# Two PSUM buffers in turn for the query, gate and attention products of a fused attention and feed-forward block

## What is computed

```python
x = x + _layernorm(attn(_layernorm(x)))
x = x + _layernorm(ffn(_layernorm(x)))

def attn(x):                        # 16 heads of 64
    q = elu(x @ Wq + bq) + 1;  k = elu(x @ Wk + bk) + 1;  v = x @ Wv + bv
    kv = einsum('bhsd,bhse->bhde', k, v)     # 64 x 64 for each head
    a = einsum('bhsd,bhde->bhse', q, kv)
    return (sigmoid(x @ Wg + bg) * a) @ Wo + bo
```

## Time and profile before

| | us |
|---|---|
| median of the 2 runs | 8979.28 |
| the two runs | 8975.19, 8983.37 |
| the profiled execution | 8972.89 |
| its span on the slowest core (core 4) | 8971.4 |
| its spans on the 8 cores | 8903.2 to 8971.4 |

### The profile page before, as it was taken

The page is one execution under the profiler, slowest core; times in us unless marked ns, Lnnn a source line. Parts: engine busy times, 40 slices in busy tenths (PEclk is TensorE's granted clock), DMA queues, the critical chain, the costliest instruction groups (busy, mean ns, idle before and its releaser), DMA issues.

```text
span 8971.4 us, 65942 instructions; the slowest of 8 cores (8903.2 to 8971.4 us)
## 1 busy us (share of the span) xinstructions
PE 3763.7 (42%) x20044; PEld 2064.9 (23%) x20044; DVE 2859.9 (32%) x5319; ACT 1023.5 (11%) x1615; POOL 386.6 (4%) x214
## 2 busy tenths in 40 slices
PE   0246566563767667765232213222332132213221
PEld 0122222222444444443111111111111111111110
DVE  4521211213222222222433343234323432343333
ACT  0211111110111111111001010101010101010101
POOL 0200000000000000000000000000000000000000
PEclk9987777776888888887666667665756676667676
DMA  6610000002000000001232223222322232223221
GB/s 187 198 51 19 19 24 19 21 22 75 19 24 29 29 29 27 17 29 38 63 85 62 57 51 85 63 57 49 85 59 59 52 85 61 59 50 85 61 61 45
DMA packets 679993, 495.11 MB, mean 55 GB/s; under 512 B 561891, under 2 KB 561891, under 8 KB 677606
## 3 DMA queue, kind: packets, MB, share of 16 engines
q1 hardware_dynamic: 660198, 423.78, 17.9%
q0 software_dynamic: 19456, 67.12, 2.1%
HBM read 423.71 MB, written 67.11 MB: 55 GB/s over the span
## 4 chain that ended last, share of the span: by engine, by line
PE 35%; DVE 26%; DMA 17%; issue 9%; ACT 8%; POOL 3%; DVEq 2%; SPq 0%; ACTq 0%; POOLq 0%
DMA w2qs<-w2q 7%; DMA w1qs<-w1q 6%; PE pq L724 5%; PE pk L520 5%; PE po L822 4%; PE pg L759 4%; PE ph L1244 4%; PE pv L520 4%; POOL H L1131 3%; DVE H L1051 3%; DVE H L1048 3%; ACT H L1057 2%; PE po2a L1165 2%; DVE H L1043 2%; PE po2b L1165 2%
## 5 line engine op out<-in xcount | busy, mean ns | idle before, releaser
L1244 PE MATMUL ph<-xqT,w1qs 128*128 128x256 bf16 x4096 | 571.4, 303 | 351.0 <-DMA w1qs<-w1q 317.9
L1165 PE MATMUL po2a<-w2qs,hqb 128*128 128x512 bf16 x1024 | 374.3, 453 | 791.1 <-DMA w2qs<-w2q 400.0
L1090 PE MATMUL pbcst<-identf,cmaxb 128*128 128x128 f32 x64 | 28.6, 447 | 1483.9 <-DVE cmaxb L1084 1454.5
L1244 PEld LDWEIGHTS ph<-xqT,w1qs 128*128 128x128 bf16 x4096 | 428.1, 108 | 494.1 <-issue 406.8
L1253 DVE TENSOR_TENSOR H<-ph,invB 128x256 f32<-128x256 f32 x512 | 217.6, 425 | 701.6 <-PE ph L1244 701.2
L1131 POOL TENSOR_TENSOR H<-H,sc2B 128x8192 f32<-128x8192 f32 x16 | 257.2, 16076 | 3032.8 <-DVEq L109 3032.8
L1165 PE MATMUL po2b<-w2qs,hqb 128*128 128x512 bf16 x1024 | 384.3, 464 | 0.0
L1185 DVE TENSOR_SCALAR ffnb<-po2a,fac2c 128x1024 f32<-128x1024 f32 x16 | 20.5, 1284 | 1071.2 <-PE po2b L1165 1071.2
L1090 PEld LDWEIGHTS pbcst<-identf,cmaxb 128*128 128x128 f32 x64 | 11.7, 182 | 1500.8 <-issue 1500.8
L724 PE MATMUL pq<-xh_b,wq_h 128*128 128x256 f16 x1024 | 169.8, 321 | 408.5 <-DVE qf L737 328.2
L1014 PE MATMUL pbcst<-diagb,onesf 128*128 128x128 f32 x64 | 24.5, 487 | 712.1 <-DVE diagb L1010 712.1
(11 more groups left out here) (206 smaller groups left out, 6969.1 us busy)
## 6 DMA issues: line engine op xcount, KB each, us to landing
w1qs<-w1q SPq DMA_DIRECT2D x256, 512.0 KB, 4.4
w2qs<-w2q SPq DMA_DIRECT2D x512, 256.0 KB, 2.6
qstage<-w SPq DMA_DIRECT2D x64, 512.0 KB, 4.4
qstage<-w SPq DMA_DIRECT2D x16, 2048.0 KB, 9.9
xin<-x SPq DMA_DIRECT2D x32, 512.0 KB, 3.6
xr_b<-x SPq DMA_DIRECT2D x32, 512.0 KB, 4.3
x<-x_b POOLq DMA_DIRECT2D x32, 512.0 KB, 5.9
x2in<-x SPq DMA_DIRECT2D x16, 1024.0 KB, 5.3
```

What stands on the lines that cost most here:

```text
L1165: last = t.matmul(out=PO2[tl][:, half * 512:(half + 1) * 512], lhsT=hqb[:, s, tl * 128:(tl + 1) * 128], rhs=w2qs[:, wb, half * 512:(half + ...
L1244: last = t.matmul(out=pb[:, :], lhsT=w1qs[:, (s // 2) % 2, s % 2, c, :], rhs=xqT[:, buf, c, :], start=(c == 0), stop=(c == 7))
```

## The change

Each of the three tiles `pq`, `pg` and `pa` becomes two tiles, and the chunks take them in turn (`fo % 2`, `pr % 2`). The free event is kept for each tile, so a chunk waits for the readers of the chunk two before it and no longer of the one before it. Nothing else is changed: the same instructions stand in the same order in all five lists. PSUM tiles are placed by whole banks of 2 KB; phase 2 had 3 tiles in one bank each and `po` in two, and has 6 and two after.

```diff
-        pq = ps2("pq", [128, 256])
-        pg = ps2("pg", [128, 256])
-        pa = ps2("pa", [128, 256])
+        pq2 = [ps2("pq0", [128, 256]), ps2("pq1", [128, 256])]
+        pg2 = [ps2("pg0", [128, 256]), ps2("pg1", [128, 256])]
+        pa2 = [ps2("pa0", [128, 256]), ps2("pa1", [128, 256])]
...
-        pq_free = Res()
-        pg_free = Res()
-        pa_free = Res()
+        pq_free = [Res(), Res()]
+        pg_free = [Res(), Res()]
+        pa_free = [Res(), Res()]
...
+                pq = pq2[fo % 2]
...
-                p.op("tensor", q_mm, wait=[t_xT, t_wqgo] + pq_free.wait(), inc=[s_qmm2.inc()])
+                p.op("tensor", q_mm, wait=[t_xT, t_wqgo] + pq_free[fo % 2].wait(), inc=[s_qmm2.inc()])
...
-                pq_free.freed_by((s_qch, s_qch.v))
+                pq_free[fo % 2].freed_by((s_qch, s_qch.v))
...
+                pg = pg2[fo % 2]
...
-                p.op("tensor", g_mm, wait=[t_xT, t_wqgo] + pg_free.wait(), inc=[s_gmm.inc()])
+                p.op("tensor", g_mm, wait=[t_xT, t_wqgo] + pg_free[fo % 2].wait(), inc=[s_gmm.inc()])
...
-                pg_free.freed_by((s_gch, s_gch.v))
+                pg_free[fo % 2].freed_by((s_gch, s_gch.v))
...
+                pa = pa2[pr % 2]
...
-                p.op("tensor", a_mm, wait=[t_q, t_kv] + pa_free.wait(), inc=[s_amm.inc()])
+                p.op("tensor", a_mm, wait=[t_q, t_kv] + pa_free[pr % 2].wait(), inc=[s_amm.inc()])
...
-                pa_free.freed_by((s_gav, s_gav.v))
+                pa_free[pr % 2].freed_by((s_gav, s_gav.v))
```

More of the change, by code:

```diff
@@ L718, in build_nc, with q_mm @@
             for fo in range(8):
-                def q_mm(t, fo=fo, buf=buf):
+                pq = pq2[fo % 2]
+                def q_mm(t, fo=fo, buf=buf, pq=pq):
                     last = None
@@ L728, in q_mm @@
                     return last
-                p.op("tensor", q_mm, wait=[t_xT, t_wqgo] + pq_free.wait(), inc=[s_qmm2.inc()])
+                p.op("tensor", q_mm, wait=[t_xT, t_wqgo] + pq_free[fo % 2].wait(), inc=[s_qmm2.inc()])
                 t_qmm = (s_qmm2, s_qmm2.v)
-                p.op("vector", lambda v, fo=fo: v.tensor_scalar(
+                p.op("vector", lambda v, fo=fo, pq=pq: v.tensor_scalar(
                     out=qtmp[:, :], in0=pq[:, :], scalar1=bqcol[:, fo:fo + 1], scalar2=0.0,
@@ L753, in build_nc, with g_mm @@
             for fo in range(8 if KP2SUB >= 2 else 0):
-                def g_mm(t, fo=fo, buf=buf):
+                pg = pg2[fo % 2]
+                def g_mm(t, fo=fo, buf=buf, pg=pg):
                     last = None
@@ L763, in g_mm @@
                     return last
-                p.op("tensor", g_mm, wait=[t_xT, t_wqgo] + pg_free.wait(), inc=[s_gmm.inc()])
+                p.op("tensor", g_mm, wait=[t_xT, t_wqgo] + pg_free[fo % 2].wait(), inc=[s_gmm.inc()])
                 t_gmm = (s_gmm, s_gmm.v)
-                p.op("scalar", lambda sE, fo=fo: sE.activation(
+                p.op("scalar", lambda sE, fo=fo, pg=pg: sE.activation(
                     out=gT[:, fo, :], in_=pg[:, :], func=AF.Sigmoid, bias=bgcol[:, fo:fo + 1],
@@ L769, in build_nc, with a_mm @@
                     wait=[t_gmm] + gT_free[fo].wait(), inc=[s_gch.inc()])
-                pg_free.freed_by((s_gch, s_gch.v))
+                pg_free[fo % 2].freed_by((s_gch, s_gch.v))
             xTb_free[buf].freed_by((s_qmm2, s_qmm2.v), (s_gmm, s_gmm.v))
             for pr in range(8 if KP2SUB >= 3 else 0):
-                def a_mm(t, pr=pr):
+                pa = pa2[pr % 2]
+                def a_mm(t, pr=pr, pa=pa):
                     c0 = pr * 128
@@ L789, in a_mm @@
                                     tile_position=(64, 64))
-                p.op("tensor", a_mm, wait=[t_q, t_kv] + pa_free.wait(), inc=[s_amm.inc()])
+                p.op("tensor", a_mm, wait=[t_q, t_kv] + pa_free[pr % 2].wait(), inc=[s_amm.inc()])
                 t_amm = (s_amm, s_amm.v)
-                p.op("vector", lambda v, pr=pr: v.scalar_tensor_tensor(
+                p.op("vector", lambda v, pr=pr, pa=pa: v.scalar_tensor_tensor(
                     out=qf32[:, pr, :], in0=pa[:, :], scalar=1.0, in1=gT[:, pr, :],
```

## The result

| | before | after |
|---|---|---|
| median of the runs, us | 8979.19 (10 runs) | 8484.37 (11 runs) |
| ratio after / before | | 0.944, 95% interval 0.941 to 0.947 |
| the profiled execution's span, us | 8971.4 | 8475.9 |
| mean of its spans on the 8 cores, us | 8949.4 | 8449.2 |

The change makes the kernel 5.6% faster. This and every later ratio leaves out executions in which the cores of one die ran at a lower clock than the others and took longer (2 of the 11 of the changed kernel, 8605 and 8743 us).

What follows compares the result with a forecast made beforehand. Waits bound the kernel, no engine being busy for half the span. Gains of 15 x 32.2 + 30.5 = 513 us, taken from 8972.9, give 8459.9; the runs' median lies 6.4 higher: 8466 us, range 8425 to 8570.

Steps and rivals of the forecast that it cites:

- Chunk 2 starts where chunk 1 did, slowly: Q stage: chunk 2 still waits for the LN in VectorE's queue, starting at 3090.53; TensorE idles 5.6 us instead of 8.11.
- VectorE is the bound from there at 3.28 us: Q stage from chunk 2's data on: VectorE's chain takes 3.28 us a chunk, of which TensorE works 2.62.
- Full clock from chunk 3: Q stage: TensorE runs at 2.4 GHz from chunk 3 on, 2.62 us a chunk.
- Bound (a): Q stage, clock of chunk 3: at 1.2 GHz VectorE starts it 2.1 us later, +34 us; chunk 2 already fast, -5 us.
- bound (b): Q stage: one more slow chunk in the steady part costs 1.8 us, +29 us in all.
- The a stage keeps VectorE's pace: A stage: 8 x 1.45 us and about 0.2 us, 11.8 us against 13.1 or 13.4; gain 1.4 us an iteration.
- The o stage stays as it is: O stage: unchanged, since its own wait concerns po, which is not doubled; no gain or loss.
- Bound (c): O stage start: if a shorter a stage kept the clock up, about 2.2 us would be won, -35 us in all.
- A (q stays slow): Rival, q stage: stays at 1.2 GHz, 5.1 us a chunk; 8645 us; chance 0.10 including cases between it and the forecast.
- B (no gain): Rival, q and g stages: denser work is granted 1.2 GHz throughout; 8960 us, or 8979 us; chance 0.05.
- C (slower): Rival: q, g and o stages all at 1.2 GHz, 18 us more an iteration in o; about 9250 us; chance 0.03.
- D (the clock sags in part): Rival: a quarter of g and o matmuls at 1.2 GHz, 9.5 us an iteration, 152 us; 8618 us; chance 0.03.

Runs made afterwards that it cites:

- two casts: The changed kernel with VectorE's cast into q_hb done three times instead of once in each q chunk: ratio 0.948 to the kernel before.
- filled gaps: The kernel before, single tiles, with extra matmuls into an unread PSUM tile behind q chunks 0 to 6: 8888 us against 9014, ratio 0.983.
- later profile: The changed kernel run again unaltered, as base for other runs: 8521 us against 9041 for the kernel before, ratio 0.944.
- `pq` alone: The changed kernel with only pq doubled, pg and pa single again: 8687 us against 9014 for the kernel before, ratio 0.962.
- mixed a stage: The changed kernel with its six tiles as one pool and attention products placed between g chunks: 8339 us against 9041 before, ratio 0.917.
- `pa` alone: The changed kernel with only pa doubled, pq and pg single again: 8989 us against 9014 for the kernel before, ratio 0.996.
- `pg` alone: The changed kernel with only pg doubled, pq and pa single again: 8877 us against 9014 for the kernel before, ratio 0.984.

## Why the prediction was right, step by step

All times here are put on the iteration of the timeline of after: its first q matmul at 2947.05 stands for 3079.64 in the prediction, 132.59 us earlier.

- *Chunk 2 starts where chunk 1 did, slowly.* Forecast 2957.94, measured 2957.95; idle 5.6 us forecast, 5.49 measured; its end forecast 2962.8, measured 2963.01.
- *VectorE is the bound from there at 3.28 us.* It starts at 2963.26 where 2963.0 was forecast, then at 2966.54 and 2969.82: 3.28 us. The two casts show that it is the bound and not only a match.
- *Full clock from chunk 3.* 1.00 in the window; the slow rows are of chunk 2 alone. Bound (a) and bound (b) did not occur here. (Bound (a) was summed a little high: 3095.4 + 5.1 + 0.24 is 1.8 us behind 3098.9, not 2.1.) The sign "granted clock of the q stage above 0.9" was just missed: 0.89 for the stage as a whole, because of chunk 2 and the idle time ahead of it. That the clock follows the gaps, which the prediction took from the comparison of q and g, is shown by the filled gaps.
- *The g stage has no wait.* Forecast 2977.3 to 2998.5, measured 2977.60 to 2998.73.
- *The a stage keeps VectorE's pace.* The first L795 forecast at 2999.36, measured at 2999.59; the pace is 1.45 us. The o stage starts at 3011.83 and not at 3011.16: 0.2 us are inherited, and in this iteration VectorE loses 0.46 us before its last operation.
- *Reading one tile while the other is written costs nothing.* The first read of `pq` takes 0.48 us before and after. The term put at nothing was nothing.
- *The o stage stays as it is.* Not quite, and this is the largest miss in the sum. Bound (c), a faster start, did not come true; the start is slower. The first eight matmuls take 3.57 us as in the earlier trace rows, but the second eight of the iteration read take longer, before (core 4) and after (core 6):

```profile
3056.17 2.44 PE L822 MATMUL po<-wo_l,gav_h 128*128 128x512 f16 x8
```

```profile
3015.20 2.91 PE L825 MATMUL po<-wo_l,gav_h 128*128 128x512 f16 x8
```

The forecast was built on one iteration of each stage. The means of 14 iterations (the second to the fifteenth, same cores; us, rounded) show what that cost:

| from first start to first start | before, the iteration used | before, mean | after, forecast | after, mean |
|---|---|---|---|---|
| q stage | 53.2 | 53.2 | 30.3 | 30.7 |
| g chunks 0 to 6 | 26.1 | 26.6 | 18.3 | 18.4 |
| g chunk 7 and a stage | 17.0 | 16.9 | 15.5 | 15.6 |
| o stage | 26.8 | 26.9 | 26.8 | 27.4 |
| iteration | 123.2 | 123.6 | 91.0 | 92.1 |

The iteration after is 1.1 us longer than forecast: 0.4 us in the q stage, 0.5 in the o stage, where the trace has 5.6 us at 1.2 GHz against 4.6 before, and 0.1 in the a stage. But the mean iteration before is 0.5 us longer than the one used, mostly because 4 of 16 g stages restart slowly. The two misses partly cancel, and that is luck: the gain is 31.5 us and not 32.2. The first iteration, put at 30.5 us with half of the late start as a guess, gave 30.0 (mean start of its o stage over the cores, 2308.2 us before and 2278.2 after). Together that is 10 us less than the forecast of 513. The other 8 us between 8466 and 8484 are no step of the sum; they are less than what phase 3 differs by between cores and runs.

*The rivals.* A (q stays slow) is refuted by `pq` alone and the window. B (no gain) and C (slower) by the result. D (the clock sags in part) was set aside too firmly. In the profiled execution of after it is not there, but in the same kernel's later profile six cores had it in this stretch, two of them for a quarter of the time, see the last section. The figure that the Trainium skill (TensorE: Matmul & The Clock Gate, Part 1) gives for it, 13/16, is the level that the later profiles show, and the row of phase 1 that I held against it, 216 ns a matmul, shows only that it does not always come: the profiled executions of before and after have no time at 0.81 on any core.

## What to carry to other kernels

A single PSUM tile between TensorE and a slow chain costs twice: the waits themselves, and the clock that they bring down; the second was half of the gain of the q stage here. Price a second buffer by rebuilding one iteration: the pace becomes that of the slower engine's whole chain (3.28 us), not of TensorE's 2.62, and what stands ahead in the reader's queue (the LN, 5.5 us) stays until the buffers are deeper. Buffers of stages that follow one another can be one pool: the same six banks in one rotation gave another 10 us an iteration, with no instruction more.

## What the runs showed of the hardware

**The gap and the clock.** A granted clock of 0.75 with idle times of 2.1 us and more between chunks, 1.00 with 0.37 us (filled), 0.5 us (after) and 0.77 us (g stage before). A lone gap of 2.23 us was followed by 16 matmuls at 1.2 GHz in every iteration of `pq` alone; one of 2.05 us in the same place of the kernel before was followed by full clock in 12 of 16 iterations, and so was the gap of 2.47 us at 3117.05. So a gap of about 2 us does not bring the clock down each time, and where the limit lies was not measured. Matmuls whose result nobody reads paid for themselves.

**A granted clock of 0.81 on some cores in some executions.** In the kernel with the mixed a stage, one execution, 2710 to 2720 us after each core's own start, core 6 and then core 2, and two matmul rows of core 6:

```profile
2710.00:2720.00 10.00, 10.00 (x78) 8.27 (x77) 6.25 (x15) 1.56 (x4) 0.00 (x0) 0.81 0.61 206
```

```profile
2710.00:2720.00 10.00, 10.00 (x94) 8.97 (x92) 6.48 (x16) 1.25 (x3) 0.00 (x0) 1.00 0.56 193
```

```profile
2714.36 1.23 PE L730 MATMUL pp<-xl_b,wq_h 128*128 128x256 f16 x8
2715.41 1.22 PE L730 MATMUL pp<-xh_b,wq_l 128*128 128x256 f16 x8
```

Eight matmuls are 1.05 us apart on core 6, 131 ns each, where they are 109 ns at full clock. Of the merged rows of eight q or g matmuls, core 6 had 448 of 728 like this and core 2 none.

The trace also has the granted clock of each core over time, so its share in the o-to-o stretch can be added up. In the changed kernel's later profile the clock was at 0.81 for 387 us of 1451 on core 2, 393 of 1445 on core 3, 160 to 177 of 1414 and 1411 on cores 0 and 1, 113 to 117 on cores 4 and 5, and never on cores 6 and 7 (1403 us); the window of 2300 to 3600 us, core 2 and then core 6:

```profile
2300.00:3600.00 1300.00, 1093.53 (x7414) 728.70 (x7412) 447.50 (x1069) 252.64 (x403) 14.92 (x28) 0.85 0.11 35
```

```profile
2300.00:3600.00 1300.00, 1076.23 (x7578) 724.00 (x7578) 460.23 (x1098) 258.02 (x411) 15.46 (x29) 0.89 0.11 36
```

The kernel with `pa` alone, hardly denser than the one before, had it for 287 of 1888 us on core 0, so it does not need a dense kernel. The profiled executions of before, of after and of the kernel with two casts had it on no core.

It looks as if it came for a pair of cores (0 and 1, 2 and 3, ...), but the traces say otherwise. No core waits for another, and each core's times count from its own start. In the kernel with `pg` alone, core 6 had its first four episodes at 529, 741, 839 and 1149 us and core 4 had four at 6594, 6806, 6905 and 7214 us: always 6065 us later. All nine episodes of core 6 match core 4 or 5 in this way. One of them, core 6 and then core 4:

```profile
840.00:853.00 13.00, 11.95 (x45) 4.27 (x43) 0.80 (x1) 0.00 (x0) 0.00 (x0) 0.81 0.00 0
```

```profile
6905.00:6918.00 13.00, 8.26 (x60) 5.93 (x57) 2.98 (x7) 0.00 (x0) 0.00 (x0) 0.81 0.74 161
```

In the six other profiles that have 0.81 a die's episodes match too, with one shift of 0.6 to 5.3 ms between its two pairs and none within a pair: at that shift 70 to 98% of one core's time at 0.81 falls into the other's episodes, where 3 to 19% would by chance. The plain reading, an inference from the matches, is that the die went to 0.81 as a whole while its pairs of cores were at different places of the program, having started that far apart. What a pair loses in phase 2 then depends on when it started.

The Trainium skill (TensorE: Matmul & The Clock Gate, Part 1) has a limiter to 13/16 = 0.8125 for dies on which three or more cores are dense. The level agrees, and that it takes the whole die agrees with the matching episodes. That it needs three dense cores was tested by no run here. The densest kernel lost most: its stretches were 1198 to 1299 us by core, so a part of what a denser TensorE wins is at risk.
